# Angular factors in PSUM for the outer product of a graph convolution, and a ring of four PSUM banks for the steps' sums

## The reference, cut to what matters

```python
src = node_in[edge_src]                       # one row of 256 for each edge
s0, s1 = src[:, :64], src[:, 64:].reshape(-1, 64, 3)
a0, a1 = edge_attr[:, 0:1], edge_attr[:, 1:4]
out0 = alpha * (einsum(s0 * a0, w_00_0) + inv_sqrt3 * einsum('eim,em,io->eo', s1, a1, w_11_0))
out1 = alpha * (einsum('ei,io,em->eom', s0, w_01_1, a1) + einsum(s1 * a0, w_10_1))
messages = concat(out0, out1) * msg_rad       # msg_rad: one factor for each edge
agg = segment_sum(messages, edge_dst)         # added up for each destination node
```

## Time and profile before

| | |
|---|---|
| median of 3 runs | 3231.2 us (3222.32 to 3235.33) |
| the profiled execution | 3236.17 us, span 3234.4 us |
| convolution, first gather to last addition | 1824.4 to 2456.5 us of the span |
| busy in the whole span | PE 2370.8, DVE 2013.8, POOL 1807.8, ACT 1366.3 us |
| mean granted clock of TensorE | 0.842 |

### The profile page before, as it was taken

How to read it: one execution, slowest core, us unless ns; L and a number is a source line. 1 busy time by engine, 2 the same in 40 slices (tenths; PEclk the granted TensorE clock), 3 DMA queues, 4 the chain that set the end, 5 groups by cost and what they waited for, 6 DMA issues and landing times. The chain is left out here.

```text
span 3234.4 us, 41071 instructions
## 1 busy us (share of the span) xinstructions
PE 2370.8 (73%) x11128; PEld 1542.6 (48%) x11128; DVE 2013.8 (62%) x4084; ACT 1366.3 (42%) x3768; POOL 1807.8 (56%) x1789
## 2 busy tenths in 40 slices
PE   0898677777776366679987677777777788888781
PEld 0455455555554266236643333332235667776661
DVE  3544799999998986100136288888886452222588
ACT  0122556565562144231125388878884122222230
POOL 1243788788782056527763377777772237777200
PEclk9899878888887655589988788888889879999895
DMA  5000766766760000323422133333330131111104
GB/s 120 23 33 26 218 201 201 208 201 204 208 195 24 4 2 2 98 78 117 121 52 62 53 93 95 97 93 92 95 94 21 17 73 35 35 35 38 20 1 170
DMA packets 163816, 287.79 MB, mean 89 GB/s; under 512 B 55320, under 2 KB 99357, under 8 KB 163598
## 3 DMA queue, kind: packets, MB, share of 16 engines
q0 software_dynamic: 79568, 187.15, 21.2%
q1 hardware_dynamic: 68628, 75.89, 7.6%
q10 hardware_dynamic: 15402, 22.14, 2.0%
HBM read 248.79 MB, written 36.25 MB: 88 GB/s over the span
## 5 line engine op out<-in xcount | busy, mean ns | idle before, releaser
L2282 POOL DMA_INDIRECT cv_x<-x_tab,e_src x440 | 481.4, 1094 | 197.3 <-issue 89.6
L2295 PE MATMUL cv_ps<-cv_msg,cv_hot 128*128 128x512 f32 x880 | 464.3, 688 | 166.9 <-DVE acc L2345 149.3
L926 POOL DMA_INDIRECT at_kv<-kv_tab,e_src x440 | 472.5, 1074 | 149.4 <-issue 93.7
L1982 POOL DMA_INDIRECT pairs<-gating_pair,gating_place x288 | 278.9, 968 | 247.8 <-DVE gating_place L1947 93.2
L2295 PEld LDWEIGHTS cv_ps<-cv_msg,cv_hot 128*128 128x128 f32 x880 | 189.6, 221 | 441.3 <-DVE cv_msg L2334 210.5
L2714 POOL DMA_INDIRECT gs_h<-h_tab,fc_q x312 | 296.7, 951 | 178.0 <-issue 91.1
L2308 ACT ACTIVATE cv_msg<-cv_x,factors 128x64 f32<-128x64 f32 x1320 | 356.4, 333 | 0.0
L2345 DVE TENSOR_TENSOR acc<-acc,cv_ps 128x256 f32 x880 | 297.3, 414 | 2.7 <-DVE acc L2345 2.1
L2306 ACT ACTIVATE cv_msg<-cv_x,factors 128x256 f32<-128x256 f32 x440 | 217.6, 495 | 163.9 <-DMA cv_x<-x_tab,e_src 163.9
L1062 PE MATMUL at_a<-at_kv,at_hot_e 128*128 128x264 f32 x880 | 251.7, 415 | 6.9 <-DVE at_kv L1135 5.0
L1037 PE MATMUL at_q<-q_parts,at_hot_n 128*128 x1320 | 216.2, 316 | 41.5 <-DVE at_kv L1119 34.2
(11 more groups left out here) (537 smaller groups left out, 4662.9 us busy)
## 6 DMA issues: line engine op xcount, KB each, us to landing
x_w<-in_L_ffn_w SPq DMA_DIRECT2D x16, 1024.0 KB, 8.0
at_rel_row<-e_rel_rows SPq DMA_DIRECT2D x55, 256.0 KB, 4.5
experts_out<-gs_y ACTq DMA_DIRECT2D x20, 512.0 KB, 2.7
x_y<-experts_out SPq DMA_DIRECT2D x20, 512.0 KB, 4.9
at_kv<-kv_tab,e_src POOLq DMA_INDIRECT x440, 3.9
cv_x<-x_tab,e_src POOLq DMA_INDIRECT x440, 2.8
kv_tab<-p_qkv SPq DMA_DIRECT2D x25, 256.0 KB, 2.0
gs_h<-h_tab,fc_q POOLq DMA_INDIRECT x312, 2.4
```

Of the source, the lines that this page charges most:

```text
L926: nc.gpsimd.indirect_dma_start(out=kv[:, t % (RING * Q4), 0:2 * D], out_offset=None, in_=kv_tab, in_offset=bass.IndirectOffsetOnAxis(ap=e. ...
L1982: nc.gpsimd.indirect_dma_start(out=pairs, out_offset=bass.IndirectOffsetOnAxis(ap=place_i[:, c:c + 1], axis=0), in_=pair[:, c, :], in_offs ...
L2282: nc.gpsimd.indirect_dma_start(out=xg[:, i % RT, u, :], out_offset=None, in_=x_tab, in_offset=bass.IndirectOffsetOnAxis(ap=e.src[:, t:t + ...
L2295: nc.tensor.matmul(ps[u][:, :], hot[:, i % 2, u, :], msg[:, i % 2, u, :], start=True, stop=True).then_inc(summed, 1)
```

## The change

Two edits, both in `convolve`.

- The factors are copied once, by a DVE copy of 128 x 2048 columns at the start of the stage, to `held`, a PSUM tensor that fills four banks. DVE waits for that copy, and its outer product then reads the factors 1 to 3 there in place of SBUF. ACT goes on reading them from SBUF.
- The other four banks are a ring for the sums: step t uses bank t modulo R = 4 (before: modulo 8), and its matmul waits for the additions of step t - 4 (before: t - 8).

```diff
+        R = 4
+        ps = [s.ps(f"cv_ps{u}", [P, 512]) for u in range(R)]
+        held = s.ps("cv_factors", [P, G1 * P, 4])
+        kept = s.sem("cv_kept")
...
                         pe.wait_ge(scaled, t + 1)
-                        if i:
-                            pe.wait_ge(added, 2 * (t - U) + 2)
-                        nc.tensor.matmul(ps[u][:, :], hot[:, i % 2, u, :], msg[:, i % 2, u, :], start=True, stop=True).then_inc(summed, 1)
+                        if t >= R:
+                            pe.wait_ge(added, 2 * (t - R) + 2)
+                        nc.tensor.matmul(ps[u % R][:, :], hot[:, i % 2, u, :], msg[:, i % 2, u, :], start=True, stop=True).then_inc(summed, 1)
...
-                    weights = wide(factor[:, i * U:(i + 1) * U, 1:4].unsqueeze(3), S)
+                    weights = wide(held[:, i * U:(i + 1) * U, 1:4].unsqueeze(3), S)
                     v.tensor_tensor(s1w[:, :, :, :], xg[:, i % RT, :, M:D].rearrange("p u (m i) -> p u m i", m=3), weights,
                                     ALU.mult).then_inc(freed, 1)
...
-                            v.tensor_tensor(row, row, ps[u][:, n * D:(n + 1) * D], ALU.add).then_inc(added, 1)
+                            v.tensor_tensor(row, row, ps[u % R][:, n * D:(n + 1) * D], ALU.add).then_inc(added, 1)
+                v.tensor_copy(held[:, :, :], factor[:, :, :]).then_inc(kept, 1)
+                dve.wait_ge(kept, 1)
                 build(0)
```

More of the change, by code:

```diff
@@ L2269, in convolve @@
         s1w = s.sb("cv_s1w", [P, U, 3, M])
-        ps = [s.ps(f"cv_ps{u}", [P, 512]) for u in range(U)]
+        R = 4
+        ps = [s.ps(f"cv_ps{u}", [P, 512]) for u in range(R)]
+        held = s.ps("cv_factors", [P, G1 * P, 4])
+        kept = s.sem("cv_kept")
         freed, built, chain, summed, added, scaled = (s.sem("cv_" + q) for q in ("freed", "built", "chain", "summed", "added", "scaled"))
```

## The result

The changed kernel takes 3201.75 us (median of four, 3198.56 to 3208.52), the kernel before 3228.95 beside it (3222.32 to 3235.33). The ratio is 0.9923, with a 95% interval of 0.9908 to 0.9938: 25 us faster by the ratio, 27 by the medians. The profiled execution took 3201.74 us (span 3200.0, mean granted clock 0.85), against 3236.17 for the one of before. The experiments further down were run in four sittings, each on another chip; in the first three every kernel took 11 to 13% longer because engines paused, which e7 shows and doesn't explain (the kernel before 3601 to 3649 us), so each run is compared with the kernel before of its own sitting.

The account below looks back on a forecast made before the run. POOL, its gathers lengthened by DVE operations, was taken to pace the stage: 54 x (11.2 - 10.7) = 27 us less, against 1.5 for last additions and 1.5 for the start, net -24: 3207 us, range 3190 to 3235.

Parts of the forecast that it names:

- The outer product's hold: POOL's gathers under DVE's outer product: its factors in PSUM free them, 0.73 us a turn, some 40 us in the stage.
- rival B: POOL's gathers stay held under the outer product, turn still 11.2 us: 0 to +6 us, 3234 us; chance 0.13.
- The other holds: Gathers held under DVE's comparison, 0.2 us a turn, and under its two short sums, 0.25 us.
- the step for the two sums: Gathers under DVE's two short sums: hold averaged evenly over 1.257 us between issues, 0.125 us each, 0.25 for both.
- The copy: Stage start: DVE's copy of the factors takes 2.3 us, hidden in DVE's idle time; taken 0, bounds 0 to +2.3.
- the clock's mix: PE's bursts: half the turns delay DVE by 0, four tenths by 1.6, a tenth by 2.8 us; mean 0.9.
- A: PE's mix of short and long bursts stays, DVE's turn of 10.95 us bounds: -5 us, 3226 us; chance 0.17.
- C: PE's clock falls in every turn, slowing DVE: up to a 12.45 us turn, +67 us, 3298 us; chance 0.10.
- the lighter mix: PE's bursts: shorter turns make idle times of 3.4 us rare, short and long bursts alternate; delay 0.9 instead of 1.30 us.
- Gather side: POOL's turn of eight gathers: 10.06 us undisturbed plus holds of 0.2 and 0.25, 10.5 us (10.3 to 11.4).
- DVE's side: DVE's turn: 9.65 us without any wait plus 0.9 of waiting for PE, 10.55 us.
- the 0.15 us added for unevenness: Turn of the stage: 0.15 us over the larger of POOL's 10.5 and DVE's 10.55, as uneven turns don't fully average out.

Follow-up runs that it names:

- e7: The kernel before, unedited, profiled on a third chip where engines paused: 3604.68 us, median of the sitting 3601.38 us.
- e9: The kernel before with three more gathers a turn, rows unused, for which ACT and DVE wait: 3446.45 us, ratio 1.067 to the kernel before.
- e10: The changed kernel with three more gathers a turn, rows unused, for which ACT and DVE wait: 3407.06 us, ratio 1.0558 to the kernel before.
- e8: The changed kernel, unedited, on the third chip where engines paused: 3614.38 us, ratio 1.004 to the kernel before.
- e2: The changed kernel with seven banks for sums and one for factors, the first 128 steps' factors serving all: 3643.77 us, ratio 0.9993 to the kernel before.
- e12: The changed kernel, comparison's row in PSUM, DVE reordered: outer product two turns ahead between additions 0-3 and 4-7: 3179.32 us, ratio 0.9849 to the kernel before.
- e11: The changed kernel, comparison's row in PSUM, two more products of constants a turn behind the fourth matmul: 3178.89 us, ratio 0.9845 to the kernel before.
- e4: The changed kernel with the comparison's row of 128 numbers also read from PSUM: 3652.46 us, ratio 1.0038 to the kernel before.

## Why the prediction was right, point by point

**The outer product's hold.** Forecast: 40 us of excess go with the operand's move to PSUM. It fell from 40.0 us to nothing (0.949 to 0.957 us for the 64 gathers under it), and rival B is out: the gathers' busy sum is 448.2, inside 435 to 450. In e9 and e10, where POOL paces alone, the turn gets 0.66 us shorter with all holds counted (0.73 was the forecast for the outer product's alone). The Trainium skill ("SBUF — State Buffer", Who interferes with whom) says that a DVE instruction with one SBUF input doesn't contend with GpSimd; the trace agrees, with 0.95 us for gathers under an outer product. The same section's inference that a tensor_tensor, with both inputs in SBUF too, leaves descriptor generation alone fails again: 1.78 us under the comparison.

**The other holds.** Forecast 0.2 us a turn for the comparison and 0.25 for the two sums, 0.45 together. Measured 24.4 us in all (0.44 a turn) and 4.5 us (0.08), 0.52 together; the comparison's was 11.7 us before. The sum came out nearly right, its two terms didn't: POOL and DVE don't meet at an even spread of phases, as the step for the two sums assumed; they run almost in step, and it seems that the comparison, which comes first, now takes what the outer product took (the phases themselves weren't varied). The term mis-sized is the 0.2 that was carried over unchanged.

**The outer product's own time and the copy.** No change was forecast (0 to +0.1 us): 1747 ns against 1759. The copy was put at 2.3 us, hidden, and not in POOL's way:

```profile
1816.60 2.29 DVE L2349 COPY cv_factors<-factors 128x2048 f32<-128x2048 f32 x1 [0.52 <-PEq L2203]
1817.20 0.96 POOL L2285 DMA_INDIRECT cv_x<-x_tab,e_src  x1 [61.64 <-SPq L2276]
1818.46 0.95 POOL L2285 DMA_INDIRECT cv_x<-x_tab,e_src  x1 [0.30 <-issue]
```

It takes 2.29 us, and the gather that lies wholly beside it 0.96. The 1.5 us set against the start didn't come: 11.9 us to the first outer product, 12.0 before.

**The ring of four.** The forecast of the clock's mix was half, four tenths and a tenth for delays of 0, 1.6 and 2.8 us, 0.9 in the mean. Of the 55 bursts 28 take 7.1 us, 21 take 8.5 to 8.8 and 4 take 10.1 (the first has only four products, the last twelve), and the additions of a turn take 6.35 us in place of 5.45: 0.90. So neither A (a mix as before, 1.30) nor C (a delay in every turn) happened; the additions' wait for PE is 35.3 us, at the lower end of 35 to 60. The Trainium skill names cycling through PSUM banks, with short idle times between groups of products, as a thing that makes the clock oscillate ("TensorE: Matmul & The Clock Gate", A second HAM failure mode). The trace agrees that it oscillates, with four banks as with eight; a worse clock with four banks, for which the prediction took it in C, isn't seen (0.91 after 0.86 between 2000 and 2300 us).

The reason given for the lighter mix holds in part. Idle times of PE of 3.4 us and more, which stand ahead of all thirteen bursts of the 10 us kind in the trace of before, fell from 24 to 4 of 54. But PE's mean idle time hardly moved (2.77 to 2.72 us), and the 3.6 us expected behind a short burst didn't come: mostly it is 2.5 to 2.6 there, since such a turn takes 9.6 us, not 10.7. Of the 54 idle times 44 are 2.5 to 2.7 us, ahead of short and long bursts alike, so the idle time just ahead doesn't tell the two apart; short bursts follow short ones in nine cases, where the forecast had them alternate. The mean of 0.9 is right, and what decides the single burst stays open.

**The turn.** Gather side 10.06 + 0.52 = 10.58 us (forecast 10.5), DVE's side 9.56 to 9.65 + 0.90 (forecast 10.55), and the turn 10.64 (10.7). By the prediction's own numbers the gather side would be 10.04 (8 x 1.255); 10.06 is right with the unrounded 0.953 + 0.305. Two sides so close leave little waiting: POOL issues without a pause from the first gather to the last (447.2 us of issues and 439 x 0.305 of gaps between them make 581.1 of 581.0), and DVE has 11 us of waiting left behind its first turn. So the stretch from the first gather to the last, forecast at about 588 us, is POOL's side alone: the ring of gathered rows, four turns deep, took up all of DVE's late turns, and the 0.15 us added for unevenness wasn't needed there. 54 turns gave 31.0 us where 27 were forecast; the last additions gave back 1.2 (forecast 1.5).

**The sum.** In the stage -30 against a forecast of -24; in the medians 3201.75 against 3207, and 3190 to 3235 holds it. The profiled span has 4.4 us more of gain outside the stage, which belongs to no part of the change. What no step of the prediction had is that its premise, POOL as what paces the stage, holds for some chips only: where the engines pause as in e7, the same change costs 0.4%. What is paid there is DVE's waiting for PE, as in C, but without C's falling clock (granted clock of the stage 0.79 in e7, 0.83 in e8). Whether the ring of four by itself costs anything where nothing pauses wasn't measured; that DVE's turn with it (10.5) stays under the 11.2 of the held gathers, and that 103.0 us of its waits cost e10 nothing, speak for no cost.

What else stays open: on the chips with pauses the parts don't add up. The ring alone costs 29 to 40 us, the whole change 13, so the factors in PSUM would be worth 16 to 27 (numbers of different chips); with seven banks (e2) they and the ring together change the time by -2.6 us (-11 to +6).

## What to carry to other kernels

When POOL's indirect transfers pace a stage, look at what DVE runs beside each of them: in the traces of this case each gather that an operation with both inputs in SBUF held ended about 0.82 us after it, and one broadcast operand moved to PSUM frees it at no cost to the operation (1747 ns against 1759). The banks can be paid for by ordering DVE's queue so that half of the matmuls run under work that doesn't need them, as in e12, where the additions never wait for PE. And before resting a forecast on who paces a stage, ask how near the second one is: here it was 1.55 us a turn away before the change (9.65 against 11.2) and some 0.1 after it, and on another chip, with pauses, DVE was the nearer bound.

## What the runs showed of the hardware that was not expected

- The pauses of e7: PE, ACT and DVE idle for microseconds by "issue" and "remote" on three of the experiments' four chips, 3601 to 3649 us in place of 3227, with the same kernel.
- TensorE's clock was higher with products of constants: 0.97 granted in e11 against 0.91, with 45 of the bursts at 7.1 us in place of 28, for 43 us more of busy PE in 300. Reordering went with as much without them, 0.99 in e12, where PE runs four matmuls at a time with 1.05 and 1.67 us between them.
- A hold removed can move to another operation of the same kind: the comparison's grew from 11.7 to 24.4 us when the outer product's 40.0 went, and fell away with its own operand in PSUM (gathers' busy sum 428.2 us in e4, 423.2 in e12, of which 419.3 are 440 undisturbed gathers). It need not: in e10 the comparison's fell with it, from 5.5 us in e9 to 0.8, and that of the sums stayed (10.5 and 10.9).
